# Two transposed-input tensors placed at the far end of the SBUF partitions in a fused attention and feed-forward kernel

## The chip, the cores and the metric

The kernel runs on one core of one Trainium2 chip. The metric is the device time of one execution in microseconds (us). The kernel before has three timed executions, whose median counts.

## The reference, cut to what matters

One transformer block over 4 sequences of 256 rows with 512 features: a modulated layer norm, a gated linear attention with 32 query heads in 8 groups, its output projection, a second modulated layer norm and a gated feed-forward network with 1376 inner features.

```python
h = _layernorm(x, axis=-1) * (1 + ca) + sa
q = (h @ Wq.T)            # 32 heads of 128, rotated
k, v = h @ Wk.T, h @ Wv.T # 8 heads of 128
...                       # chunks of 128 rows: scores * decay, y = intra + inter
y = y / rms * gnorm_w
gate = (h @ Wg.T)
x = x + ga * ((y * (gate * sigmoid(gate))) @ Wo.T)
h = _layernorm(x, axis=-1) * (1 + cb) + sb
x = x + gb * ((silu(h @ w_gate.T) * (h @ w_up.T)) @ w_down.T)
```

## The kernel before, in words

TensorE (PE) has a fast mode for float32 operands that were rounded first (type float32r). So the kernel keeps each operand as a rounded part `hi` and a rest `lo` and adds three products, w_hi·x_hi, w_hi·x_lo and w_lo·x_hi, in `three_products` (lines 54, 55, 56; the profile gives each matmul one of these lines). Only the scores and y products (lines 659, 668, 673, 679) and some small ones run on plain float32.

`hT_hi` and `hT_lo` hold the transposed, normalised input h: 128 partitions by 4 feature tiles by 1024 rows each, 16384 bytes a partition. They are the *moving* operand (the one that is streamed through the array column by column) of four families of matmuls:

- `ps_q` and `ps_gt`: the query and gate projections of one head and one half of the rows, 12 matmuls of 512 columns in a block (`q_block`, `g_block`), 64 blocks of each;
- `ps_fg` and `ps_fu`: the gate and up projections of the feed-forward network, 512 columns each, the first inner tile in parts of 256;
- `ps_d`: the down projection. There the projected input is no longer needed, and `old_hi`, `old_lo` reuse the bytes of hT_hi and hT_lo for eight of the eleven tiles of its weights: the profile calls those matmuls `ps_d<-hT_hi,...`. The other three tiles lie in d0_hi/d0_lo (tile 0) and d_hi/d_lo (tiles 9 and 10); the profile calls all three `d_hi`, `d_lo`, since it leaves numbers out.

In `ps_kv` they are the *stationary* operand (the one that is loaded into the array), and wkv_hi and wkv_lo move, 256 columns at a time. In `ps_o` (wo_hi, wo_lo moving, z_hi, z_lo stationary) and `ps_ss` (sq_hi, sq_lo moving, a tensor of ones stationary) they have no part.

```python
OLD = KT * B * L // HID
old_hi, old_lo = (h[:].rearrange("p k (m n) -> p (k m) n", n=HID) for h in (hT_hi, hT_lo))

def d_tile(k, first, old, new):
    return first[:] if k == 0 else old[:, k - 1] if k <= OLD else new[:, k - 1 - OLD]
```

The order of the work is written out by hand. In the attention each engine runs a loop over seven groups of heads whose body is eight steps `step(g, t, ...)`, one for each tile of 128 rows, and then an eighth group in straight code; in each step PE does the scores, a q block, an output product, the y product, three quarters of a g block, the sum of squares, the last quarter, and in even steps a kv batch. The down projection does tiles 0 and 1 of the output together and then tiles 2 to 7 one by one, each with k from 0 to 10. Engines meet by semaphores, and each wait is written out; memory is given out by a stack of tensors, in the order in which the code names them, so a tensor's address is the sum of what was named before it.

Of the kernel before, what the change touches and what calls it, by code (L numbers as in the profile page):

```python
# [7 lines left out]
F32 = mybir.dt.float32  # L8
F32R = mybir.dt.float32r

P = 128
B, L, HID = 4, 256, 512
# [5 lines left out]
KT = HID // P  # L18
# [40 lines left out]
def build(nc, x_in, cT_in, wmod_in, wq_in, wg_in, wkv_in, wo_in, win_in, rows_in, gnorm_in,  # L59
          wgu_in, wd_in, cst_in, out):  # L60
    modrow = nc.dram_tensor("modrow", (2, B * HID), F32, kind="Internal").ap()
    gT_dram = nc.dram_tensor("gT_dram", (H, B * L), F32, kind="Internal").ap()

    with ExitStack() as outer:
        def sb(name, shape, dt=F32):
            return outer.enter_context(nc.sbuf_tensor(name, shape, dt))

        cst = sb("cst", [P, C_TRI])
        x1 = sb("x1", [P, NT, HID])
        hT_hi = sb("hT_hi", [P, KT, B * L], F32R)  # L70
        hT_lo = sb("hT_lo", [P, KT, B * L], F32R)
        tok = sb("tok", [P, NT, 3, H])
        modT = sb("modT", [P, 4, KT, B])
        gnorm = sb("gnorm", [P, 1])
        raw_pair = sb("raw_pair", [P, KT, 2 * P])
        norm_rows = [sb("stats", [P, NT, 6]), sb("mv", [P, NT, 2]), sb("var", [P, NT]),
                     sb("rstd", [P, NT])]
        ident = cst[:, C_ID:C_ID + P]

        block_attention(nc, cst, x1, hT_hi, hT_lo, tok, modT, gnorm, ident, modrow, gT_dram,  # L80
                        x_in, cT_in, wmod_in, wq_in, wg_in, wkv_in, wo_in, win_in, rows_in,
                        gnorm_in, cst_in, wgu_in, norm_rows, raw_pair)
        block_ffn(nc, x1, hT_hi, hT_lo, modT, ident, modrow, wgu_in, wd_in, out, norm_rows,
                  raw_pair)
# [1604 lines left out]
```

## Time and profile before

| | |
|---|---|
| three timed executions | 1119.6, 1121.64, 1122.24 us; median 1121.64 us |
| the profiled execution | 1125.82 us, of which the span from first to last instruction is 1124.0 us |
| granted TensorE clock, mean | 0.983 of full |
| busy | PE 96%, weight loads 72%, VectorE (DVE) 68%, ScalarE (ACT) 49%, GpSimd (POOL) 18% |

The busy time of PE is modelled at its end: a matmul of 512 columns is shown some 395 ns long and overlaps the next, so its price in a dense stream is the distance from one start to the next. The timeline gives starts to 10 ns; a mean over many matmuls in a row is finer than that.

### The profile page before, as it was taken

The page shows a single profiled execution, that of the slowest core. Times are in us where ns is not written, and L with a number is a line of the kernel's source. Part 1 is how long each engine was busy: PE and PEld are TensorE (multiplying, and loading weights), DVE is VectorE, ACT ScalarE, POOL GpSimd, SP SyncE. Part 2 cuts the span into 40 slices and gives each one's busy share as a digit, 9 for nine tenths or more (in the row PEclk, how much of TensorE's full clock was granted, in tenths as well). Part 3 has the DMA queues.
Part 4 walks back from the last instruction along what each step waited for, and adds up shares of the span by engine and source line. Part 5 has one row for each costly group of instructions (what it writes and reads, how often), then busy time and mean ns, then how long its engine had stood idle before and what let it go on. Part 6 is the DMA issues. An engine that isn't in the chain of part 4 may idle for free. (4 is left out here: it accounts for less than half of the span.)

```text
span 1124.0 us, 14213 instructions
## 1 busy us (share of the span) xinstructions
PE 1078.1 (96%) x4680; PEld 808.6 (72%) x4680; DVE 768.3 (68%) x1492; ACT 550.6 (49%) x1133; POOL 206.4 (18%) x131
## 2 busy tenths in 40 slices
PE   5869999999999999999999999999999969999898
PEld 1747777777777777777777777777776448888676
DVE  5777876877788678868877887778676785444411
ACT  2445555666555566555666555666555434222300
POOL 2412121211222121122111221211121530000000
PEclk8989999999999999999999999999999989999999
DMA  6111311220131013102201310131030431111011
GB/s 221 48 52 56 121 38 37 83 77 19 37 112 37 19 37 112 37 27 82 95 19 37 103 46 19 37 112 37 19 106 22 192 130 40 56 37 57 29 38 37
DMA packets 37464, 70.89 MB, mean 63 GB/s; under 512 B 2936, under 2 KB 19576, under 8 KB 35520
## 3 DMA queue, kind: packets, MB, share of 16 engines
q1 hardware_dynamic: 36720, 70.16, 19.3%
q10 hardware_dynamic: 720, 0.43, 0.1%
q8 instruction: 13, 0.21, 0.1%
q14 instruction: 11, 0.09, 0.0%
HBM read 68.33 MB, written 2.24 MB: 63 GB/s over the span
## 5 line engine op out<-in xcount | busy, mean ns | idle before, releaser
L1299 POOL TENSOR_TENSOR q_sin<-q_sin,cst 128x512 f32<-128x512 f32 x64 | 83.0, 1296 | 395.8 <-ACT q_sin L751 395.8
L1292 POOL TENSOR_TENSOR dec<-dec,future 128x1024 f32<-128x1024 f32 x31 | 80.3, 2591 | 273.8 <-ACT expg L770 273.8
L54 PE MATMUL ps_gt<-hT_hi,wg_hi 128*128 128x512 f32 x256 | 126.4, 494 | 3.6 <-DVE sg L986 3.6
L848 ACT ACTIVATE work<-ps_y 128x512 f32<-128x512 f32 x64 | 38.3, 598 | 186.1 <-PE ps_y L673 185.3
L54 PE MATMUL ps_q<-hT_hi,wq_hi 128*128 128x512 f32 x256 | 126.5, 494 | 2.8 <-DVE q_cos L966 2.3
L54 PE MATMUL ps_o<-wo_hi,z_hi 128*128 128x512 f32 x260 | 104.1, 400 | 2.4 <-DVE z_lo L49 2.4
L56 PE MATMUL ps_o<-wo_hi,z_lo 128*128 128x512 f32 x260 | 103.1, 396 | 0.0
L55 PE MATMUL ps_o<-wo_lo,z_hi 128*128 128x512 f32 x260 | 102.7, 395 | 0.0
L55 PE MATMUL ps_gt<-hT_lo,wg_hi 128*128 128x512 f32 x256 | 101.9, 398 | 0.0
L56 PE MATMUL ps_q<-hT_hi,wq_lo 128*128 128x512 f32 x256 | 101.9, 398 | 0.0
L56 PE MATMUL ps_gt<-hT_hi,wg_lo 128*128 128x512 f32 x256 | 101.8, 398 | 0.0
L55 PE MATMUL ps_q<-hT_lo,wq_hi 128*128 128x512 f32 x256 | 101.5, 396 | 0.0
L750 ACT ACTIVATE q_sin<-ps_q 64x512 f32<-64x512 f32 x64 | 38.1, 595 | 113.8 <-PE ps_q L56 113.7
L49 DVE TENSOR_TENSOR sq_lo<-work,sq_hi 128x512 fp32r<-128x512 f32 x64 | 45.6, 713 | 61.9 <-ACT sq_hi L849 61.9
L780 ACT ACTIVATE dec<-dec,scal 128x128 f32<-128x128 f32 x256 | 81.8, 403 | 1.4 <-DVE scal L944 1.4
L1160 DVE SCALAR_TENSOR_TENSOR work<-ps_s,scal,dec 128x128 f32<-128x128 f32 x240 | 67.5, 344 | 20.7 <-DVE z_lo L49 11.1
L1190 DVE TENSOR_TENSOR work<-work,rms 128x512 f32<-128x512 f32 x64 | 44.4, 694 | 53.2 <-ACT rms L857 53.2
L966 DVE TENSOR_TENSOR q_cos<-ps_q,cst 128x512 f32<-128x512 f32 x64 | 44.1, 689 | 43.8 <-ACT q_sin L751 43.8
L54 PE MATMUL ps_kv<-wkv_hi,hT_hi 128*128 128x256 f32 x256 | 73.2, 286 | 0.0
L56 PE MATMUL ps_kv<-wkv_hi,hT_lo 128*128 128x256 f32 x256 | 72.7, 284 | 0.0
L55 PE MATMUL ps_kv<-wkv_lo,hT_hi 128*128 128x256 f32 x256 | 72.2, 282 | 0.0
L659 PE MATMUL ps_s<-qT,kT 128*128 128x512 f32 x128 | 65.6, 593 | 3.4 <-DVE qT L974 3.4
(239 smaller groups left out, 2537.9 us busy)
## 6 DMA issues: line engine op xcount, KB each, us to landing
dec<-gT_dram SPq DMA_DIRECT2D x32, 512.0 KB, 5.4
raw_q<-wq_in SPq DMA_DIRECT2D x32, 256.0 KB, 2.6
raw_g<-wg_in SPq DMA_DIRECT2D x32, 256.0 KB, 2.9
raw_o<-wo_in SPq DMA_DIRECT2D x8, 1024.0 KB, 7.0
raw_pair<-wkv_in SPq DMA_DIRECT2D x8, 512.0 KB, 4.6
raw_pair<-wgu_in SPq DMA_DIRECT2D x6, 512.0 KB, 3.3
raw_gu<-wgu_in SPq DMA_DIRECT2D x5, 512.0 KB, 3.3
qT<-wmod_in SPq DMA_DIRECT2D x2, 1024.0 KB, 7.0
```

The lines of the kernel that those rows point to most:

```text
L49: return engine.tensor_tensor(lo, full, hi.bitcast(F32), ALU.subtract)
L54: pe.matmul(out, w_hi, x_hi, start=first, stop=False)
L55: pe.matmul(out, w_hi, x_lo, start=False, stop=False)
L56: return pe.matmul(out, w_lo, x_hi, start=False, stop=last)
L659: nc.tensor.matmul(ps_s[:].rearrange("p (h i) -> p h i", h=GRP), kT[:, b % 2, c * P:(c + 1) * P], qT[:, half, :, rows_of(t)], start=True, ...
L780: last = nc.scalar.activation(cell, cell, ACT.Exp, bias=scal[:, bn * CPB + c, 0, h:h + 1])
L848: nc.scalar.activation(sq, ps_y[:], ACT.Square).then_inc(sq_done, 1)
L966: nc.vector.tensor_tensor(q_cos[:].rearrange("p (b i) -> p b i", b=2), ps_q[:].rearrange("p (b i) -> p b i", b=2), cosT, ALU.mult)\
L1160: last = nc.vector.scalar_tensor_tensor(dest[:, h], ps_s[:, h * P:(h + 1) * P], scal[:, t, 1, h:h + 1], dec[:, b % 2, h, c], ALU.mult, ALU ...
L1190: nc.vector.tensor_tensor(z[:], z[:], rms[:].rearrange("p (h i) -> p h i", h=GRP), ALU.mult).then_inc(z_done, 1)
L1292: nc.gpsimd.tensor_tensor(cells, cells, future[:].unsqueeze(1).broadcast_to([P, GRP * CPB, CHUNK]), ALU.add).then_inc(mask_done, 1)
L1299: nc.gpsimd.tensor_tensor(q2, q2, sinT, ALU.mult).then_inc(qsin_done, 1)
```

## The change

```diff
-        def sb(name, shape, dt=F32):
-            return outer.enter_context(nc.sbuf_tensor(name, shape, dt))
+        def sb(name, shape, dt=F32, side=None):
+            return outer.enter_context(nc.sbuf_tensor(name, shape, dt, side=side))
 
         cst = sb("cst", [P, C_TRI])
         x1 = sb("x1", [P, NT, HID])
-        hT_hi = sb("hT_hi", [P, KT, B * L], F32R)
-        hT_lo = sb("hT_lo", [P, KT, B * L], F32R)
+        hT_hi = sb("hT_hi", [P, KT, B * L], F32R, "right")
+        hT_lo = sb("hT_lo", [P, KT, B * L], F32R, "right")
```

First byte of the tensors in each partition, as the built programs have them:

| tensor | bytes | before | after |
|---|---|---|---|
| cst, x1 | 4608, 16384 | 16512, 21120 | the same |
| hT_hi | 16384 | 37504 | 212960 |
| hT_lo | 16384 | 53888 | 196576 |
| wq_hi, wg_hi | 8192 each | 78048, 94432 | 45280, 61664 |
| wkv_hi, wkv_lo | 4096 each | 110816, 114912 | 78048, 82144 |
| wo_hi, wo_lo | 8192 each | 119008, 127200 | 86240, 94432 |
| sq_hi, sq_lo | 2048 each | 200288, 202336 | 167520, 169568 |
| z_hi, z_lo | 2048 each | 206432, 208480 | 173664, 175712 |
| ones_r | 512 | 216672 | 183904 |
| a_hi, a_lo (feed-forward) | 45056 each | 78048, 123104 | 45280, 90336 |
| d0_hi, d0_lo | 2048 each | 180448, 182496 | 147680, 149728 |
| wgu_hi, wgu_lo | 8192 each | 192736, 200928 | 159968, 168160 |
| d_hi, d_lo (down projection) | 4096 each | 192736, 196832 | 159968, 164064 |

## Rows read from the trace of the kernel before

**Rows 1.** The page, first lines: busy time, share of the span, instructions.
```profile
span 1124.0 us, 14213 instructions
PE 1078.1 (96%) x4680; PEld 808.6 (72%) x4680; DVE 768.3 (68%) x1492; ACT 550.6 (49%) x1133; POOL 206.4 (18%) x131
```

**Rows 2.** Windows: stretch, busy time of each engine (instructions), granted clock, DMA.
```profile
200.00:400.00 200.00, 200.00 (x880) 151.07 (x880) 152.98 (x309) 116.25 (x239) 40.11 (x23) 1.00 0.17 52
400.00:600.00 200.00, 200.00 (x886) 151.57 (x885) 153.62 (x310) 115.31 (x237) 41.39 (x24) 1.00 0.19 58
940.47:1052.90 112.43, 112.43 (x482) 90.22 (x480) 44.13 (x58) 24.61 (x40) 0.00 (x0) 1.00 0.13 43
```

**Rows 3.** Groups by shape, PE: how many matmuls; busy, mean ns; idle before.
```profile
L54 PE MATMUL ps_q<-hT_hi,wq_hi 128*128 128x512 f32 x256 | 126.5, 494 | 2.8 <-DVE q_cos L966 2.3 <-DVE wq_lo L49 0.5
L54 PE MATMUL ps_gt<-hT_hi,wg_hi 128*128 128x512 f32 x256 | 126.4, 494 | 3.6 <-DVE sg L986 3.6
L54 PE MATMUL ps_o<-wo_hi,z_hi 128*128 128x512 f32 x260 | 104.1, 400 | 2.4 <-DVE z_lo L49 2.4
...
L54 PE MATMUL ps_kv<-wkv_hi,hT_hi 128*128 128x256 f32 x256 | 73.2, 286 | 0.0
...
L54 PE MATMUL ps_fg<-hT_hi,wgu_hi 128*128 128x512 f32 x80 | 31.7, 397 | 0.0
...
L54 PE MATMUL ps_d<-hT_hi,a_hi 128*128 128x512 f32 x64 | 25.5, 398 | 0.0
```

**Rows 4.** Timeline, PE, feed-forward: first and last of 480 matmuls of 512 columns.
```profile
940.47 0.40 PE L54 MATMUL ps_fg<-hT_hi,wgu_hi 128*128 128x512 f32 x1
...
1052.70 0.39 PE L56 MATMUL ps_fu<-hT_hi,wgu_lo 128*128 128x512 f32 x1
```

**Rows 5.** Timeline, PE, down projection: 24 matmuls from hT, 9 from d, the next from hT.
```profile
1089.95 0.40 PE L54 MATMUL ps_d<-hT_hi,a_hi 128*128 128x512 f32 x1
...
1095.57 0.40 PE L54 MATMUL ps_d<-d_hi,a_hi 128*128 128x512 f32 x1
...
1096.03 0.39 PE L56 MATMUL ps_d<-d_hi,a_lo 128*128 128x512 f32 x1
...
1097.62 0.40 PE L54 MATMUL ps_d<-hT_hi,a_hi 128*128 128x512 f32 x1
```

**Rows 6.** Timeline, PE, one loop step: gate block, squares, kv batch, q block, output product.
```profile
299.67 0.39 PE L55 MATMUL ps_gt<-hT_lo,wg_hi 128*128 128x512 f32 x1
...
301.53 0.39 PE L686 MATMUL ps_ss<-sq_hi,ones_r 128*128 128x512 f32 x1
301.76 0.39 PE L688 MATMUL ps_ss<-sq_lo,ones_r 128*128 128x512 f32 x1
301.99 0.39 PE L54 MATMUL ps_gt<-hT_hi,wg_hi 128*128 128x512 f32 x1
...
302.68 0.28 PE L54 MATMUL ps_kv<-wkv_hi,hT_hi 128*128 128x256 f32 x1
...
305.43 0.28 PE L56 MATMUL ps_kv<-wkv_hi,hT_lo 128*128 128x256 f32 x1
...
306.64 0.40 PE L55 MATMUL ps_q<-hT_lo,wq_hi 128*128 128x512 f32 x1
...
309.21 0.39 PE L54 MATMUL ps_o<-wo_hi,z_hi 128*128 128x512 f32 x1
```

**Rows 7.** Timeline, PE, last group: first and last of 12 output-product matmuls.
```profile
894.98 0.40 PE L54 MATMUL ps_o<-wo_hi,z_hi 128*128 128x512 f32 x1
...
897.55 0.39 PE L56 MATMUL ps_o<-wo_hi,z_lo 128*128 128x512 f32 x1
```

**Rows 8.** Timeline, DVE, same step as in the loop: the tightest hand-over to PE.
```profile
300.75 0.69 DVE L49 TENSOR_TENSOR sq_lo<-work,sq_hi 128x512 fp32r<-128x512 f32 x1 [0.53 <-ACT sq_hi L849]
```

**Rows 9.** Groups by shape, DVE: the same work on tensors in different places.
```profile
L1190 DVE TENSOR_TENSOR work<-work,rms 128x512 f32<-128x512 f32 x64 | 44.4, 694 | 53.2 <-ACT rms L857 53.2
L1594 DVE TENSOR_TENSOR res<-res,x 128x512 f32<-128x512 f32 x8 | 5.5, 692 | 0.3
```

## The prediction

> **What bounds the kernel now.** I read the page first: PE is busy for 96% of the span, the next engine, DVE, for 68% [rows 1]. Then the windows: in the middle of the attention PE is busy in 200.00 of 200.00 us, twice, at a granted clock of 1.00 (the level of 2.4 GHz), with DVE at 153 us and ACT at 116 us; in the feed-forward stretch PE is busy in 112.43 of 112.43 us and DVE in 44 us [rows 2]. So for most of the span nothing is waited for, and only the price of PE's own matmuls counts. No instruction differs between the two programs, so all hangs on one question: does that price depend on where an operand lies?
>
> The groups do not answer it, since the end of a matmul is modelled: 397 to 400 ns are shown for every family in the dense stretches, and the 494 ns of lines 54 in the projections only holds the one start in four that follows a plain float32 product [rows 3]. The timeline does, by starts. I divide the distance of two starts by the number of matmuls between them, all of 512 columns unless said.
>
> - Feed-forward, moving from hT: 479 distances in 1052.70 - 940.47 = 112.23 us, 234.3 ns each [rows 4].
> - Down projection, moving from hT's bytes: 24 in 1095.57 - 1089.95 = 5.62 us, 234.2 ns each. Then nine that move from d0 or d: 2.05 us, 227.8 ns each, and the last seven of them, once the rate has settled, 1097.62 - 1096.03 = 1.59 us, 227.1 ns each [rows 5].
> - Loop: gate block, eight in 301.53 - 299.67 = 1.86 us, 232.5 ns each; query block, eleven in 309.21 - 306.64 = 2.57 us, 233.6 ns each; sums of squares (moving sq), two in 0.46 us, 230 ns each [rows 6].
> - Output product (moving wo): eleven in 897.55 - 894.98 = 2.57 us, 233.6 ns each [rows 7].
> - kv batch, 256 columns, moving wkv, hT stationary: 23 from 302.68 to 305.43, 119.6 ns each, which is 239 ns for 512 columns [rows 6].
>
> 512 columns at 2.4 GHz would be 213.3 ns, so each float32r matmul carries 13 to 21 ns more, and how much differs by tensor. The second item is the argument. The 24 and the 9 are the same instruction on the same shapes in the same accumulation, a few hundred ns apart, with the same kind of values (weights of the down projection) in both, with weights loaded from the same two tensors a_hi and a_lo, and in every output tile alike. What differs is where the moving operand lies: hT at 37504 to 70272, d0 and d at 180448 to 200928. That is worth 234.2 - 227.1 = 7.1 ns a matmul, 3%.
>
> **What in the address matters.** Three readings fit rows 5. (a) Moving from high addresses, or from above the stationary operand, is cheaper: a lies at 78048 to 168160, below d and above hT. (b) hT starts at a multiple of 128 bytes, all the other tensors 96 past one. (c) Something that the change keeps, such as the 16384 bytes between hT_hi and hT_lo, against 2048 or 4096 in d0 and d. Output products speak against (b) alone: wo is 96 past such a multiple too, but takes 233.6 ns in rows 7; it lies at 119008 to 135392, below its stationary z at 206432, as (a) wants. The squares, moving from 200288 with ones at 216672, lie between at 230 ns. The kv batch speaks for (a) only weakly: it moves from above its stationary hT, yet pays 239 ns for 512 columns, though two matmuls of 256 are not one of 512. After the change hT is at the top of everything, above every stationary operand, and starts 96 past a multiple of 128. So both (a) and (b) make its matmuls cheap, and only (c) leaves them as they are.
>
> **The sum, if hT gets the rate of d.** Counts are from [rows 3], three lines to each group.
> - Query blocks: 64 x 12 = 768, of which 64 first ones follow a float32 product and are left at their price: 704 x (233.6 - 227.1) = 4.6 us.
> - Gate blocks: 704 x (232.5 - 227.1) = 3.8 us.
> - Feed-forward, 480 of 512 columns: 480 x (234.3 - 227.1) = 3.5 us. The 96 of 256 columns in its first tile: the trace has no cheap row of that width, so 0, at most half of 7 ns each, 0.3 us.
> - Down projection: 192 x 7.1 = 1.4 us.
> Together 13.3 us.
>
> What else moves, down by 32768 bytes: wo and z, wkv, sq, d0 and d, and every tensor of DVE, ACT and POOL. d0 and d stay at their rate, for at 147680 to 168160 they are still above a at 45280 to 135392. If instead what counts is a high address as such, they fall back to hT's old rate: 72 x 7.1 = 0.5 us given back. sq could lose 230 to 234: 128 x 4 = 0.5 us. wo keeps its order below z: nothing. wkv comes to lie below its stationary hT: its 768 matmuls might go to half of hT's rate, 234.3 / 2 = 117.2 ns against 119.6, a gain of 768 x 2.4 = 1.8 us, or lose as much; I take 0. For the vector engines the place does nothing that I can see: the addition over work and rms around 200000 takes 694 ns, that over res and x1, of which x1 lies at 21120, 692 ns [rows 9]. DMAs do not touch hT at all. With 0 to 1 us given back I take 13 us.
>
> Does PE stay the bound when it is 1.2% faster? The tightest hand-over in the loop is sq_lo: DVE has it at 300.75 + 0.69 = 301.44, PE starts the matmul that reads it at 301.76, so 0.32 us is spare [rows 6, 8]. In the 1.8 us between the y product and this matmul PE would gain 8 x 5.4 ns = 0.04 us. The cover holds, so all gains of PE count in full.
>
> The sum is against the profiled execution: 1125.8 - 13 = 1112.8 us. The profiled execution is 4.2 us above the median of the timed ones, mostly what the profile itself and the ends cost, so I take the same 13 us from the median: 1121.6 - 13 = 1108.6, and say **1109 us**.
>
> **A rule that speaks against it.** The trace shows rate differences between places on an otherwise quiet PE [rows 5]. The Trainium skill, page "SBUF — State Buffer", section "Who interferes with whom", says that the only contention in this memory is the port pair that VectorE and GpSimd share, that TensorE has separate read ports for the moving operand and the weight load, and that it never waits on anyone; it names no influence of a byte address. By that rule the change does nothing, and the time is 1121.6 us. The trace does not quite agree: the 7 ns have no place in it.
>
> **Rivals.**
> 1. *Nothing changes* (c, or the rows are governed by something else that goes with k, such as the spacing of hi and lo). For: wo sits 8192 apart, is at 233.6 ns, hT 16384 apart at 234.2, d 2048 or 4096 at 227.1, in that order too, and the spacing of hT stays. Against: no row contradicts (a). It gives 1121.6, with 0.5 us of drift by the other tensors either way. Chance 0.30.
> 2. *A part of the gain*: hT gets the rate of the squares, 230 ns, instead of 227. Then 704 x 3.6 + 704 x 2.5 + 480 x 4.3 + 192 x 4.2 = 2.5 + 1.8 + 2.1 + 0.8 = 7.2 us, less 1 given back: 1115.5 us. Or only the feed-forward and down projections gain, since in the loop blocks of 12 never settle: 4.9 us, 1117 us. Chance 0.20.
> 3. *Slower*: the price is one of the pair moving and stationary, and the far end is a bad partner for weights that now lie at 45280 to 78000 (wq, wg) or 160000 (wgu). The worst row that I have is the kv batch, 239 ns for 512 columns, with moving and stationary 41 to 81 KB apart. If all matmuls from hT fell to it: 704 x 5.4 + 704 x 6.5 + 480 x 4.7 + 192 x 4.8 = 3.8 + 4.6 + 2.3 + 0.9 = 11.6 us, 1133 us. It decides (over +0.3%, 3.4 us) from 1.6 ns a matmul up. Against: in rows 4 and 5 hT has the same 234.2 and 234.3 ns beside stationary tensors at 192736 and at 78048, so the partner seems to matter little. Chance 0.15.
>
> **The numbers.** The forecast itself, hT at or near the rate of d: 0.35, with a range of its own from 1105 to 1113. With rival 2 faster has 0.55; within 0.3%, about what a measurement of this kernel can tell from no change, 0.30; slower 0.15. The likeliest case is 1109; from 1105 up to 1124.5 the range takes in the forecast, the part gains and no change, and leaves out the slower case and a little below.
>
> **What the profile after would show.** If right: starts in the feed-forward stretch 227 ns apart instead of 234.3, so its 480 matmuls take 109 us instead of 112.4; the 24 and the 9 of the down projection at one rate; query and gate blocks near 227 to 228; kv, wo and squares within 2 ns of before; all durations of DVE and ACT the same. If the spacing rules, the 24 stay at 234.2 and the 9 at 227. If high addresses as such rule, hT goes to 227 and d to 234. I would be wrong if the seven distances after hT in rows 5 are cheap for another reason than place, since my whole sum hangs on them.

## The result and the profile after

The changed kernel takes 1113.59 us (median of five, 1113.17 to 1115.70) against 1121.64 us before: a ratio of 0.9924, 95% interval 0.9908 to 0.9940. That is 8.05 us less where 13 were forecast: faster, inside the range from 1105 to 1124.5, and 4.6 us above the point.

The page of the kernel after, its first lines; they answer to [rows 1]:

```profile
span 1111.8 us, 14213 instructions
PE 1067.2 (96%) x4680; PEld 808.9 (73%) x4680; DVE 767.0 (69%) x1492; ACT 550.8 (50%) x1133; POOL 206.1 (19%) x131
```

PE is the bound as before, in 10.9 us less of busy time. Next the timeline of PE after, feed-forward, first and last of the 480 matmuls (start, duration, both in us):

```profile
933.33 0.40 PE L54 MATMUL ps_fg<-hT_hi,wgu_hi 128*128 128x512 f32 x1
...
1041.93 0.39 PE L56 MATMUL ps_fu<-hT_hi,wgu_lo 128*128 128x512 f32 x1
```

479 distances in 108.60 us are 226.7 ns each, against 234.3 in [rows 4]: 3.6 us gone. The down projection after, nine matmuls from d, then 24 from hT, then d again:

```profile
1083.91 0.39 PE L54 MATMUL ps_d<-d_hi,a_hi 128*128 128x512 f32 x1
...
1085.95 0.39 PE L54 MATMUL ps_d<-hT_hi,a_hi 128*128 128x512 f32 x1
...
1091.39 0.39 PE L54 MATMUL ps_d<-d_hi,a_hi 128*128 128x512 f32 x1
```

2.04 us for nine and 5.44 us for 24 are 226.7 ns each. In [rows 5] it was 227.8 and 234.2; now both kinds run at one rate, though d itself has moved from 180448 and up to 147680 and up. The same step of the loop as in [rows 6], after: a q block, an output product, a gate block.

```profile
301.93 0.39 PE L55 MATMUL ps_q<-hT_lo,wq_hi 128*128 128x512 f32 x1
302.15 0.39 PE L56 MATMUL ps_q<-hT_hi,wq_lo 128*128 128x512 f32 x1
302.38 0.40 PE L54 MATMUL ps_q<-hT_hi,wq_hi 128*128 128x512 f32 x1
...
303.31 0.39 PE L55 MATMUL ps_q<-hT_lo,wq_hi 128*128 128x512 f32 x1
...
304.45 0.40 PE L54 MATMUL ps_o<-wo_hi,z_hi 128*128 128x512 f32 x1
...
307.25 0.38 PE L556 MATMUL ps_kv<-cst,kr 128*128 128x128 f32 x2
...
309.42 0.39 PE L55 MATMUL ps_gt<-hT_lo,wg_hi 128*128 128x512 f32 x1
...
311.24 0.40 PE L686 MATMUL ps_ss<-sq_hi,ones_r 128*128 128x512 f32 x1
```

The q block's eleven distances are 229.1 ns on average (2.52 us). Its last five are 1.14 us, 228 ns; six before them take 1.38 us, 230 ns. The output product still takes 233 ns (twelve in 2.80 us). The gate block has 227.5 ns (eight in 1.82 us). So in the loop the gain arrives in part. One step can flatter or hide it: over 55 steps the eleven distances of the q blocks are 233.9 ns on average before and 230.0 after, those of the gate blocks 232.4 and 229.9. Here a block's first distance, some 630 ns, is left out, since the plain float32 product before it reaches into it. The long stretch shows the whole best. Between the 2nd and the 57th sum of squares, 55 steps, the timelines of PE, first before, then after, have these ends:

```profile
108.67 0.39 PE L686 MATMUL ps_ss<-sq_hi,ones_r 128*128 128x512 f32 x1
...
819.92 0.39 PE L686 MATMUL ps_ss<-sq_hi,ones_r 128*128 128x512 f32 x1
```

```profile
104.78 0.40 PE L686 MATMUL ps_ss<-sq_hi,ones_r 128*128 128x512 f32 x1
...
812.98 0.39 PE L686 MATMUL ps_ss<-sq_hi,ones_r 128*128 128x512 f32 x1
```

711.25 us became 708.20 us. I added up the distances between starts in this stretch, each under the family of the earlier matmul:

| family in the loop stretch, us | before | after | difference |
|---|---|---|---|
| q blocks (660 matmuls) | 176.23 | 174.06 | -2.17 |
| gate blocks (660) | 175.53 | 173.91 | -1.62 |
| output product (660) | 153.28 | 153.72 | +0.44 |
| kv batches (648) | 77.42 | 77.58 | +0.16 |
| sums of squares | 25.30 | 25.55 | +0.25 |
| all | 711.25 | 708.21 | -3.04 |

The five families make 2.94 us of it, the plain float32 products and small ones 0.1.

For all 64 steps the stretch gives 3.04 x 64 / 55 = 3.5 us. With 3.6 in the feed-forward and 1.4 in the down projection (1.3 from hT, 0.1 from d; 45.04 to 43.72 and 18.03 to 17.89 us by the same sums), less 0.3 for the 96 feed-forward matmuls of 256 columns (12.92 to 13.22 us), it makes 8.2 us, against 8.05 us by the timed runs. Most of that 0.3 is not the change: the first two of the 96 take 0.57 us after and 0.35 before, since the granted clock was already at 0.50 after and still at 1.00 before; the sixth and seventh experiments, which have the same differences of address as the changed kernel, take 13.01 us. The profiled spans differ by 12.2 us; the other 4 us lie ahead of the loop stretch (108.67 and 104.78 at its start) and belong to these executions, not to the change: the second experiment below has all of the old rates, begins that stretch at 103.37 us, and is no faster than the kernel before when timed.

### The profile page after: what moved, and what is told of

It is laid out like the page before. It is cut to its first block and busy times, and to the rows that moved or that the text cites. A ratio compares the mean times of both kernels' runs of the same rounds, so it can differ in the third digit from the quotient of the medians.

```text
span 1111.8 us, 14213 instructions
## 1 busy us (share of the span) xinstructions
PE 1067.2 (96%) x4680; PEld 808.9 (73%) x4680; DVE 767.0 (69%) x1492; ACT 550.8 (50%) x1133; POOL 206.1 (19%) x131
## 5 line engine op out<-in xcount | busy, mean ns | idle before, releaser
L54 PEld LDWEIGHTS ps_gt<-hT_hi,wg_hi 128*128 128x128 f32 x256 | 48.5, 189 | 27.0 <-issue 14.4
```

Source lines behind the costliest of these rows:

```text
L54: pe.matmul(out, w_hi, x_hi, start=first, stop=False)
```

## The experiments

The theory after the result was still the forecast's: (a), the far end as such, or moving from above the stationary operand; and its rival (b), an offset of hT within a small unit. All experiments leave the instructions alone and change only addresses, with unused tensors as pads. Since the trace shows no addresses, those named here are of the built programs. The table at the end of this section has all rates.

**1. hT at the low place, shifted by 96 bytes.**

```diff
+        sb("pad_a", [P, 24])
         hT_hi = sb("hT_hi", [P, KT, B * L], F32R)
         hT_lo = sb("hT_lo", [P, KT, B * L], F32R)
+        sb("pad_b", [P, 8])
```

> hT stays at the low place, 96 bytes further up (37600 and 53984), so that it starts 96 past a multiple of 128 like all others; every tensor behind it moves by 128 bytes and keeps its offset. If the offset decides: feed-forward starts 227 ns apart instead of 234.3, down projection 227 for all, and a total as with the far end, 1113 to 1115 us. If the place (high, or above the stationary operand) decides: 234.3 ns as before, total 1121 us.

1120.01 us, ratio 0.9981 (0.9966 to 0.9996), and 232.4 ns in the feed-forward: neither value. The offset changed the rate, by 1.9 ns, so place alone is not it; but having the offset of the others within 128 bytes is not enough.

**2. hT at the far end, 96 bytes lower.**

```diff
+        sb("pad_a", [P, 24], F32, "right")
         hT_hi = sb("hT_hi", [P, KT, B * L], F32R, "right")
```

> hT at the far end, but 96 bytes lower (212864 and 196480), so that it starts on a multiple of 128 as before the change; nothing else moves. If the place decides: 227 ns in the feed-forward, total 1113 to 1114 us, as after the change. If the offset decides: 234.3 ns, total 1120 to 1122 us.

1122.85 us, ratio 1.0005 (0.9993 to 1.0016). The timeline of PE, feed-forward, first and last of 480:

```profile
934.51 0.40 PE L54 MATMUL ps_fg<-hT_hi,wgu_hi 128*128 128x512 f32 x1
...
1046.73 0.39 PE L56 MATMUL ps_fu<-hT_hi,wgu_lo 128*128 128x512 f32 x1
```

112.22 us for 479, 234.3 ns. The loop stretch takes 711.25 us, to 10 ns that of before. hT is as far up as in the changed kernel, but for 96 bytes, and all of the gain is gone. The far end has no part in it: (a) fell here; what was left of (b) had to explain the first experiment too.

**3 and 4. hT at the low place, at 64 and at 32 past a multiple of 128** (as the first, with pads of 16 and 16, and of 8 and 24 numbers).

> Low place, 64 past a multiple of 128, all others as in the first. If the place decides: 234.3 ns in the feed-forward. If the offset decides and counts to 64 bytes, 234.3 as well; if it counts to 128, 227 or a rate of its own.

> Low place, 32 past a multiple of 128. If the place decides: 234.3 ns in the feed-forward. If the offset decides and counts to 64 bytes, 227 ns; if it counts to 128, 234.3 or a rate of its own.

One execution each: 1124.5 us with 233.3 ns in the feed-forward, and 1112.79 us with 228.9 ns. In the second the kv batch, which cost 118.5 to 119.9 ns a matmul in every kernel so far, fell to 113.6. So there are more than two rates, and no offset of hT alone put them in order: hT at 224 in 256 bytes gave 226.7 ns in the changed kernel and 232.4 in the first experiment. What did was the *difference* between the start of the moving and of the stationary operand, taken in 256 bytes. (Steps inside a tensor, over k, heads and row tiles, are multiples of 512 bytes here and drop out.) It was 160 before (hT at 128, wq, wg, wgu and a at 224), is 0 after, and 128 in the first experiment, since the others had moved by 128 there. And it explained the output product, which had spoken against (b): wo and z differ by 128. The next four test it.

**5. The changed kernel, z moved by 128 bytes**, so that wo and z differ by 0.

```diff
+        sb("pad_c", [P, 32])
         z_hi, z_lo = sb("z_hi", [P, GRP, CHUNK], F32R), sb("z_lo", [P, GRP, CHUNK], F32R)
+        sb("pad_d", [P, 32])
```

> The changed kernel with z_hi and z_lo moved up by 128 bytes (and what lies behind them by 256), so that the output product's stationary operand and its moving operand wo are at the same byte in 256. If the difference of moving and stationary address, taken in 256 bytes, sets the rate: output product from 232.9 ns to 226.7, its 241 ns gone, and the query blocks behind it settled from the start, so 780 x 6 ns plus some 3 us, in all 1105 to 1108 us. If that difference is a coincidence of hT: output product 233 ns, 1113 to 1114 us.

1109.02 us, ratio 0.9880 (0.9865 to 0.9895). The timeline of PE: the first and the last matmul of one output product of the loop, and the start behind it (the added lines of code shift the line numbers a little):

```profile
314.26 0.39 PE L54 MATMUL ps_o<-wo_hi,z_hi 128*128 128x512 f32 x1
...
316.75 0.40 PE L56 MATMUL ps_o<-wo_hi,z_lo 128*128 128x512 f32 x1
316.99 1.02 PE L675 MATMUL ps_y<-work,v 128*128 128x512 f32 x2
```

Eleven distances in 2.49 us, 226.4 ns, with none of the 241 ns that two of its twelve distances had in the changed kernel. The family's sum in the loop stretch fell from 153.72 to 149.90 us and the stretch from 708.20 to 704.21. The second part of the expectation failed: the q and gate blocks did not get cheaper (173.79 and 173.97 us against 174.06 and 173.91), so their slow starts are not the output product's doing.

**6. hT at the low place at 224 in 256 bytes, all behind it moved by 256** (pads of 24 and 40 numbers around hT). **7. hT exactly where it was, all behind it moved by 160 bytes:**

```diff
         hT_lo = sb("hT_lo", [P, KT, B * L], F32R)
+        sb("pad_b", [P, 40])
```

> hT at the low place, at 224 in 256 bytes, and all behind it moved by 256, so that their bytes in 256 stay at 224 (96 for z and the squares). If the difference in 256 bytes sets the rate: 226.7 ns in the feed-forward, 120 ns in the kv batch, 1113 to 1115 us as at the far end. If the far end has a part in it: 230 ns or more, 1117 to 1122 us.

> hT exactly where it was before the change; every tensor named after it is moved up by 160 bytes, so that weights and hT are both at 128 in 256 bytes. If the difference sets the rate: 226.7 ns in the feed-forward, kv 120 ns, 1113 to 1115 us. If an address of hT of its own (its place or its offset) does: 234.3 ns, 1121 us.

1113.66 us, ratio 0.9913 (0.9898 to 0.9928), and 1112.76 us, ratio 0.9912 (0.9898 to 0.9925): the whole gain of the change both times, at the low place. The timeline of PE in the seventh:

```profile
103.19 0.39 PE L687 MATMUL ps_ss<-sq_hi,ones_r 128*128 128x512 f32 x1
...
811.14 0.39 PE L687 MATMUL ps_ss<-sq_hi,ones_r 128*128 128x512 f32 x1
...
930.72 0.40 PE L54 MATMUL ps_fg<-hT_hi,wgu_hi 128*128 128x512 f32 x1
...
1039.32 0.39 PE L56 MATMUL ps_fu<-hT_hi,wgu_lo 128*128 128x512 f32 x1
```

707.95 us for the loop stretch and 226.7 ns in the feed-forward, with not one byte of hT moved. No address of hT of its own can do that, nor one of the weights alone: they lie at 224 in 256 bytes both before (234.3 ns) and after (226.7). The difference of the two does.

**8, 9, 10. hT at the far end, lower by 64, 32 and 224 bytes** (as the second, with 16, 8 and 56 numbers).

> hT at the far end, 64 bytes lower: moving minus stationary is 192 in 256 bytes for hT's matmuls, 64 for the kv batch. Under the difference theory a fixed rate of its own in the feed-forward, not one seen so far (227 at 0, 229 at 64, 233.3 at 96, 232.3 at 128, 234.3 at 160), and the kv batch at 117.5 ns, as the 256-column matmuls of the feed-forward had at 64; total between 1108 and 1120 us. If only offset 0 is special and all others alike: 232 to 234 ns.

> hT at the far end, 32 bytes lower: moving minus stationary is 224 in 256 bytes for hT's matmuls, 32 for the kv batch. The difference theory says nothing of the size at a difference that no run had; both are a steady pattern, between 226 and 235 ns and between 113 and 121 ns. Should the near side of 0 be cheap as 64 was (229 ns), 226 to 230 ns.

> hT at the far end, 224 bytes lower: moving minus stationary is 32 in 256 bytes for hT's matmuls, 224 for the kv batch. As before, between 226 and 235 ns in the feed-forward; between its neighbours 0 (226.7) and 64 (229) if the rate goes smoothly with the difference, so 226.7 to 229 ns.

1120.44 us (ratio 0.9977, 0.9962 to 0.9992), 1116.92 and 1123.18 us (one execution each). All three give 233.3 ns in the feed-forward. So 0 is the one cheap difference of 512-column matmuls among those tried and 64 the next; the guess that a difference of 32 would lie between its neighbours 0 and 64 was wrong. The 256-column ones go another way: in the eighth the last 48 distances of those of the feed-forward are 113.3 ns each, against 120.0 in the changed kernel. There hT moves, at 192 from its stationary operand. The fourth has the same difference in its kv batch, with hT stationary and both operands on other bytes in 256. The timelines of PE, first the eighth, then one kv batch of the fourth from its 7th to its last matmul:

```profile
929.80 0.28 PE L56 MATMUL ps_fu<-hT_hi,wgu_lo 128*128 128x256 f32 x1
...
935.24 0.28 PE L56 MATMUL ps_fu<-hT_hi,wgu_lo 128*128 128x256 f32 x1
```

```profile
323.61 0.28 PE L54 MATMUL ps_kv<-wkv_hi,hT_hi 128*128 128x256 f32 x1
...
325.54 0.28 PE L56 MATMUL ps_kv<-wkv_hi,hT_lo 128*128 128x256 f32 x1
```

48 distances in 5.44 us are 113.3 ns, 17 in 1.93 us are 113.5. Read like this over all kernels, the two families have the same rate wherever they have the same difference, feed-forward first: 120.0 and 120.0 ns at 0, 116.7 and 116.7 at 32, 117.8 and 117.8 at 64, 120.0 and 120.2 at 96, 118.6 and 118.6 at 160, 113.3 and 113.4 at 192, 118.3 and 118.2 at 224; only at 128 do they part, 118.6 and 120.0. Except at 0, where some pairs share their bytes, the pairs of bytes differ each time, so here it is the difference that counts. For 512 columns that is shown at 0 alone (both operands at 224, or both at 128); every other difference was tried there on one pair of bytes.

**11 and 12. The kernel of the fifth, with wkv placed 192 in 256 bytes from hT.**

```diff
+        sb("pad_e", [P, 48])   # 112 in the twelfth
         wkv_hi, wkv_lo = (sb(n, [P, KT, 2 * D], F32R) for n in ("wkv_hi", "wkv_lo"))
+        sb("pad_f", [P, 16])
```

> The kernel with z moved by 128 bytes, and in it wkv_hi and wkv_lo at 160 in 256 bytes while their stationary operand hT stays at 224: moving minus stationary is 192, the difference at which 256-column matmuls took 113.7 ns in an earlier run. If the pair's difference sets the rate: kv batch from 119.7 to 113.7 ns, 768 x 6 = 4.6 us, 1104 to 1105 us; nothing else changes. If the cheap kv batch of that run came from the byte of hT alone: 119.7 ns, 1109 us.

> As the run before with wkv_hi and wkv_lo 256 bytes higher, so that moving minus stationary of the kv batch is 192 in 512 bytes, as in the two cheap cases (113.7 ns), and not 448 as in the run that gave 117.7 ns; in 256 bytes it is 192 in all of them. If the rate goes by 512 bytes here: 113.3 to 113.7 ns, 3 us below a kv batch at 117.7 and 4.6 us below one at 119.7, a total of 1104 to 1107 us. If it goes by 256 bytes and something else made those two cases cheap: 117.7 ns, 1108 to 1112 us.

The eleventh: 1112.05 us, ratio 0.9884 (0.9863 to 0.9906), kv batches at 117.8 ns; 1.2 us less in their sum, which the total does not show, so against the fifth it is inconclusive. The twelfth: 1107.96 us, ratio 0.9872 (0.9853 to 0.9890), the lowest of all, but its interval overlaps that of the fifth, and its kv batches average 117.6 ns: the idea of 512 bytes fell too. Its timeline shows the same kv batch of the loop body in two iterations, 102.5 us apart, so the same instructions on the same addresses, each from its 7th to its last matmul:

```profile
321.67 0.28 PE L54 MATMUL ps_kv<-wkv_hi,hT_hi 128*128 128x256 f32 x1
...
323.60 0.28 PE L56 MATMUL ps_kv<-wkv_hi,hT_lo 128*128 128x256 f32 x1
```

```profile
424.15 0.28 PE L54 MATMUL ps_kv<-wkv_hi,hT_hi 128*128 128x256 f32 x1
...
426.15 0.28 PE L56 MATMUL ps_kv<-wkv_hi,hT_lo 128*128 128x256 f32 x1
```

17 distances in 1.93 us, 113.5 ns, and 17 in 2.00 us, 117.6 ns. Of the 31 batches past the first, three keep 113.4 ns in the twelfth, one in the eleventh, 30 in the fourth. So at this difference there are two rates, and a batch keeps the one it has; that the matmuls before a batch pick it is likely, but no run shows it.

The rates, from the starts in each timeline; "512" is the feed-forward (480 matmuls, first to last), kv the mean in the loop stretch with the starts of the batches, which are not settled yet; the differences are moving minus stationary in 256 bytes:

| kernel | difference, 512 | ns, 512 | difference, kv | ns, kv | loop stretch, us |
|---|---|---|---|---|---|
| before | 160 | 234.3 | 96 | 119.5 | 711.25 |
| after | 0 | 226.7 | 0 | 119.7 | 708.21 |
| 1 | 128 | 232.4 | 128 | 119.9 | 710.33 |
| 2 | 160 | 234.3 | 96 | 119.5 | 711.25 |
| 3 | 96 | 233.3 | 160 | 118.5 | 711.45 |
| 4 | 64 | 228.9 | 192 | 113.6 | 703.99 |
| 5 (z moved) | 0 | 226.7 | 0 | 119.6 | 704.21 |
| 6 | 0 | 226.7 | 0 | 119.7 | 708.19 |
| 7 | 0 | 226.7 | 0 | 119.7 | 707.95 |
| 8 | 192 | 233.3 | 64 | 117.7 | 709.59 |
| 9 | 224 | 233.3 | 32 | 116.8 | 709.67 |
| 10 | 32 | 233.3 | 224 | 118.2 | 710.36 |
| 11 (z, wkv moved) | 0 | 226.7 | 192 | 117.8 | 703.39 |
| 12 (z, wkv moved) | 0 | 226.7 | 192 | 117.6 | 703.28 |

## Why the prediction was right, and where not

**The bound.** Right: PE had no waits in the stretches that count, and what its matmuls saved came out of the total, 8.2 us by the sums and 8.05 us timed. Taking the 13 us from the median and not from the profiled execution was sound, its reason was not: I had put the 4.2 us between the two mostly to the profile itself, but the profiled execution of the changed kernel takes 1113.59 us, exactly its median, so no run shows such a cost. The durations of the other engines did not change; DVE is busy for 767.0 us against 768.3.

**The step on which the sum hung**, that the 7.1 ns between the matmuls from hT and from d come from where the moving operand lies. Right as far as it went: hT's matmuls took d's rate in the feed-forward and the down projection, and the terms for these, 3.5 and 1.4 us, came out at 3.6 and 1.4.

**What in the address matters.** Wrong in its cause. I weighed (a), high or above the stationary operand, over (b), an offset within 128 bytes, and set (b) aside since wo shared the offset of d and was slow. The second experiment took (a) away and the seventh showed what it is: the difference of moving and stationary address in 256 bytes. The rows had it: d and a differ by 0, hT and a by 160, wo and z by 128. I had compared the addresses of the moving operands only, and had argued that the partner matters little because hT had the same rate beside two stationary tensors; those two were both at 224 in 256 bytes. The squares, whose operands differ by 0, were not cheap (230 ns), which hid this from me and is explained only in part: there are two at a time, inside a gate block, and blocks start slow. So the forecast had the sign and six tenths of the size (8.05 of 13 us) by luck: its reason would have failed at other offsets of the top, and 96 bytes lower the same change gives nothing.

**The query and gate blocks.** The terms 4.6 and 3.8 us were too large; they measured 2.17 and 1.62 us in 55 of 64 steps, 2.5 and 1.9 us in all. The step that failed is that each matmul in a block of twelve was given the settled rate. After, the q block runs on average through distances of 229 to 234 ns until the last two inside it are at 227; the gate block comes near that rate only just before the squares cut it. The averages of 230.0 and 229.9 ns stand where the sum had 227.1; the rates before, 233.6 and 232.5, were right to 0.4 ns. This is the second case of rival 2 in size: it gave 1117 us with nothing in the loop, the forecast 1109 with all of it, and the time is between, at 1113.6.

**What is given back.** 0 to 1 us was set aside; output product, kv batches and squares cost 0.85 us more in the loop stretch, and the 256-column part of the feed-forward at most 0.1 us beyond its clock.

**The rivals.** Nothing changes: excluded; the spacing of hT_hi and hT_lo, on which it rested, stayed at 16384 bytes, and hT's rate fell. Slower by a bad partner: the mechanism was nearer to the truth than the forecast's, since the price is indeed one of the pair, but the far end put hT, for 512 columns, at the best difference of all eight tried, not at a bad one. The prediction's own test, d to 234 ns if high addresses rule, was met with 226.7 ns.

**The rule of the Trainium skill**, page "SBUF — State Buffer", section "Who interferes with whom", that TensorE never waits on anyone, has no place for these runs: between the kernel before and the seventh experiment only addresses differ, and yet its loop stretch alone takes 3.3 us less (707.95 against 711.25) of a TensorE that is busy in all of it both times. Whether its two reads collide with each other, or something else depends on the pair, no run here shows.

**Left open.** Why 256 bytes, why 0 is best for 512 columns and 192 for 256 columns, what unsettles a block at its start, why the squares stay at 230 ns at a difference of 0, and what picks one of the two kv rates. That the unit is 256 and not 512 rests on the rows with 0 in 256 bytes: in the changed kernel hT and wgu differ by 256 in 512 bytes, d and a by 0, and both have 226.7 ns. Only multiples of 32 bytes were tried.

## What to carry to other kernels

Where TensorE is the bound and streams float32r operands back to back, divide the distance of the first and the last start by the number of steps between them, family by family; families of one shape that differ by a few ns are worth a look at their addresses, of both operands. Here 160 bytes of padding gave as much as the move to the far end (0.9912 and 0.9924), and the far end with 128 bytes more for the output product's pair gave 1.2% in all, at no instruction. When a placement changes a time, move each side by itself and undo it by a few bytes before naming the place as the cause.

## What the hardware showed that I had not expected

- The rate of float32r matmuls of 512 columns in a long stream, at a granted clock of 1.00 (2.4 GHz), goes with moving minus stationary address in 256 bytes: 226.7 ns at 0, 228.9 at 64, 232.4 at 128, 233.3 at 32, 96, 192 and 224, 234.3 at 160.
- At 256 columns the order is another, in settled rates of the kv batch: 113.4 ns (in 30 of 31 batches of the fourth experiment) or 117.8 at 192, 116.7 at 32, 117.8 at 64, 118.2 at 224, 118.6 at 160, 120.0 at 0 and 128, 120.2 at 96.
- It repeats: before and the second experiment have the same differences, with hT at other ends of the partition, and agree to 10 ns in 711.25 us of the loop.
- The same matmuls on the same addresses can hold one of two rates, 113.5 or 117.6 ns, for a whole batch.
